# A four-attention transformer on one core: keys, heads and norms rearranged between its attentions

## The chip, the cores and the metric

The kernel runs on one core of a Trainium2 chip. Its engines are TensorE (PE in the profile), VectorE (DVE), ScalarE (ACT), GpSimd (POOL) and SyncE (SP, which here only issues DMAs); each runs its own instruction stream, and streams meet by semaphores only. The metric is the device time of one execution in microseconds, lower is better. Time before: 2822.0 us, the median of 3 runs (2814.44 to 2823.01).

## What is computed

Two blocks of a transformer on x of shape (1024 tokens, 128), all in float32, 16 heads of 8 columns each, and a context of 6404 rows of 128. Cut to what matters:

```
x = x + cross(norm(x), ctx, mask)            # cross0: 6404 keys, masked, Wproj, bproj
z = norm(x);  a = norm(z)*g1+b1
z = z + self(a) @ Wo                         # self0: 1024 keys
t = norm(z)*g2+b2
x = x + z + top2_experts(t)                  # 8 experts, 64 hidden columns each
z = norm(x)
z = norm(self(z, causal) + z)*g1+be1         # self1
z = norm(cross(z, ctx) + z)*g2+be2           # cross1: 6404 keys, unmasked
z = norm(relu(z@Wf1+bf1)@Wf2+bf2 + z)*g3+be3
x = x + z
x = x + top2_experts(norm(x)) + shared_expert(norm(x))
```

Every attention is softmax(q kT / sqrt(8)) v by heads; every norm is over the 128 columns.

## The kernel before

Everything is written out by hand for each engine, in one block; the order of the work is the order of the code. Tokens lie on partitions in 8 tiles of 128 (x, z, xn); "turned" they lie in xT, 128 columns by 1024 tokens, in two halves of 512.

**Projections.** projection_plan lists an attention's jobs: key jobs of up to 512 columns (13 for a cross attention, 2 for a self attention), then two query jobs. Each job is one TensorE product into PSUM (project), and is then split into three bfloat16 parts that add up to the float32 value: the parts by ScalarE (L829 to 836), the rests by VectorE, the third part by GpSimd (L657, L661). SyncE stores the parts to DRAM (store_parts, L448 for keys and L452 for queries, six stores per query job) and waits for all of them (all_stored, L457). cross1's key jobs go the way called "aside", in which ScalarE copies the product and GpSimd takes the first rest too; TensorE issues them right behind self1, ScalarE runs them (split of n_k_jobs) ahead of the norm that follows self1.

**Staging.** stage loads a head's parts from DRAM into one of 4 slots of k_stages and q_stages: two sides of 64 partitions, per side three loads of keys (L469 for a cross attention, L521 for a self attention) and one or two of queries (L472, L475, L523). SyncE stages four times ahead of an attention's first pass, and then once per pass. GpSimd copies the head's values into v_stage (stage_values, L667).

**A cross attention** has 32 passes, 16 heads by 2 halves of the queries. In a pass TensorE computes the scores twice: by queries (pass_a, 28 units), from which VectorE takes maxima (take_max, L1122) out of PSUM banks 0 to 3 in turn, and by keys (pass_b), from which ScalarE takes exponentials (L925) out of banks 4 to 6; products with the values (values_step) go to bank 7. Units of pass_a run some 40 ahead of the step that needs them. A pass's negated maxima (L1132) are split by GpSimd (split_maxima, L719 to L722), turned by TensorE (turn_maxima), copied by ScalarE to max_rows and put into the query stage by SyncE (put_maxima, L483). The end of a pass: ScalarE copies bank 7 to acc_out (evacuate, L914) once the copy before has been moved, and SyncE moves it to scratch in 8 DMAs (store_out, L496). GpSimd sums the four parts of all heads (sum_first after pass 16, sum_second at the end), VectorE takes reciprocals and products into attT and marks each half as attended. The self attentions (short_attention) do two heads per pass, 16 passes; their copies (L871) go through DRAM (store_out, L545) and come back by two loads, the last one after the last pass (load_out, L552).

**Between attentions.** TensorE multiplies attT by the output weights (out_tiles) or turns it back (turn_back, for self1 and cross1, which have no output weights); VectorE adds the result; layer_norm takes statistics of all 8 tiles (L1006), var_eps (L1011), waits for ScalarE's square root (L793), and applies them (L1016), with gain and bias where there are any (L1001); turn transposes 8 tiles (L1316), and turned copies half 0 by ScalarE (L799) and half 1 by VectorE (L1028). The expert layers compute the gate (L1234 copies its logits), choose two experts, turn the coefficients and run units of 128 hidden columns by half: products for coefficients (spread) and hidden columns into PSUM, an activation, products on VectorE, and at the end the down products of all tiles (out_tiles) behind the last unit. All TensorE products stand at L1308, the helper mm. At the start GpSimd writes constants, then clears q_stages (L639) and v_stage (L643) in long memsets; after cross0 it clears the query stages again (clear_queries, L767).

## Time and profile before

| | |
|---|---|
| Runs, median of 3 | 2822.0 us (2814.44 to 2823.01) |
| The profiled execution, own time | 2820.49 us |
| its span in the profile | 2818.9 us |
| TensorE (PE), busy | 2377.8 us, 84% |
| VectorE (DVE), busy | 2337.7 us, 83% |
| ScalarE (ACT), busy | 2154.4 us, 76% |
| GpSimd (POOL), busy | 250.3 us, 9% |
| Granted TensorE clock, mean | 0.928 |

The stages, in us from the start of the span: projection of cross0 to about 95, cross0 to 1106, self0 1167 to 1346, its experts, self1 1454 to 1618, cross1 1696 to 2705, then the feed-forward layer, the last experts and the store. The busy shares are means over all of these. A row of the timeline tells when an operation began, how long it took, its engine and line, what it writes and reads, how often in a row it ran, and in brackets how long the engine had stood idle and what ended that; "SPq" is SyncE's issuing of DMAs, "PEld" the loading of weights.

### The profile page before, as it was taken

The page shows a single profiled execution, that of the slowest core. Times are in us where ns is not written, and L with a number is a line of the kernel's source. Part 1 is how long each engine was busy: PE and PEld are TensorE (multiplying, and loading weights), DVE is VectorE, ACT ScalarE, POOL GpSimd, SP SyncE. Part 2 cuts the span into 40 slices and gives each one's busy share as a digit, 9 for nine tenths or more (in the row PEclk, how much of TensorE's full clock was granted, in tenths as well). Part 3 has the DMA queues.
Part 4 walks back from the last instruction along what each step waited for, and adds up shares of the span by engine and source line. Part 5 has one row for each costly group of instructions (what it writes and reads, how often), then busy time and mean ns, then how long its engine had stood idle before and what let it go on. Part 6 is the DMA issues. An engine that isn't in the chain of part 4 may idle for free.

```text
span 2818.9 us, 58993 instructions
## 1 busy us (share of the span) xinstructions
PE 2377.8 (84%) x23115; PEld 748.0 (27%) x23115; DVE 2337.7 (83%) x2590; ACT 2154.4 (76%) x4095; POOL 250.3 (9%) x684
## 2 busy tenths in 40 slices
PE   3499999999999996498458827999999999999955
PEld 2222222222222221122222213222222222222223
DVE  7599999999999993597446438999999999999825
ACT  3189999999999996299116733999999999999941
POOL 4001101001000001000010040000000100000000
PEclk8699999999999998599669957999999999999987
DMA  4211111111111100210121131111111111111000
GB/s 140 72 31 42 35 50 44 31 40 31 28 41 30 29 19 5 68 40 23 34 68 40 51 107 38 29 41 29 29 41 29 30 41 29 31 40 28 6 5 8
DMA packets 75974, 109.23 MB, mean 39 GB/s; under 512 B 16964, under 2 KB 55672, under 8 KB 75704
## 3 DMA queue, kind: packets, MB, share of 16 engines
q1 hardware_dynamic: 73912, 101.10, 12.4%
q0 software_dynamic: 1792, 4.37, 0.9%
q8 instruction: 189, 3.10, 0.5%
q14 instruction: 81, 0.66, 0.1%
HBM read 73.93 MB, written 22.42 MB: 34 GB/s over the span
## 4 chain that ended last, share of the span: by engine, by line
PE 66%; DVE 18%; ACT 6%; SPq 4%; issue 3%; DMA 3%; POOL 1%; ACTq 0%; POOLq 0%; DVEq 0%
PE ps L1308 65%; DVE maxima L1122 12%; ACT probs L925 4%; ACT probs L881 1%; DVE maxima L1077 1%; SPq L452 1%; DVE scratch L1001 1%; POOL probs L661 1%; SPq L521 1%; DMA o_self<-acc_out 1%; DMA q_stages<-q_cross 1%; PE ps L1316 0%; DVE stats L1006 0%; DVE z L1016 0%; POOL probs L657 0%
## 5 line engine op out<-in xcount | busy, mean ns | idle before, releaser
L1122 DVE TENSOR_REDUCE maxima<-ps 128x1 f32<-128x920 f32 x1792 | 1888.8, 1113 | 102.5 <-PE ps L1308 102.5
L925 ACT ACTIVATE probs<-ps 128x512 f32<-128x512 f32 (+1 forms) x3264 | 1761.2, 594 | 146.6 <-PE ps L1308 146.2
L1308 PE MATMUL ps<-probs,v_stage 128*16 128x256 f32 x14208 | 1158.9, 393 | 0.6 <-ACT acc_out L914 0.4
L1308 PE MATMUL ps<-k_stages,q_stages 64*128 64x460 bf16 (+2 forms) x4032 | 756.3, 373 | 192.2 <-DMA q_stages<-q_cross 68.0
L1308 PE MATMUL ps<-q_stages,k_stages 64*128 64x512 bf16 (+1 forms) x3712 | 725.3, 381 | 46.0 <-ACT probs L881 18.6
L1308 PEld LDWEIGHTS ps<-k_stages,q_stages 64*128 64x128 bf16 x4032 | 193.4, 93 | 1050.0 <-issue 510.2
L1308 PEld LDWEIGHTS ps<-probs,v_stage 128*16 128x16 f32 x14208 | 236.8, 94 | 410.8 <-issue 361.4
L1077 DVE TENSOR_REDUCE maxima<-ps 128x2 f32<-128x1024 f32 (+1 forms) x224 | 240.1, 1108 | 96.1 <-PE ps L1308 92.1
L881 ACT ACTIVATE probs<-ps 128x512 f32<-128x512 f32 x448 | 224.1, 554 | 67.3 <-PE ps L1308 66.2
L1308 PEld LDWEIGHTS ps<-q_stages,k_stages 64*128 64x128 bf16 x3712 | 187.3, 93 | 279.1 <-ACT probs L925 69.8
L1001 DVE TENSOR_TENSOR scratch<-scratch 128x512 f32<-128x512 f32 x14 | 15.2, 1134 | 155.4 <-DMA scratch<-acc_out 91.1
L846 ACT ACTIVATE by_key<-ps 128x512 f32<-128x512 f32 (+1 forms) x30 | 17.5, 583 | 150.1 <-PE ps L1308 150.1
L667 POOL COPY v_stage<-by_key 128x400 f32<-128x400 f32 x64 | 33.1, 516 | 991.4 <-PE ps L1308 873.4
L793 ACT ACTIVATE std<-var_eps 128x8 f32<-128x8 f32 x9 | 1.9, 208 | 117.7 <-DVE var_eps L1011 117.7
L719 POOL CAST half_parts<-neg_max 128x4 bf16<-128x4 f32 x64 | 11.9, 186 | 852.3 <-DVE neg_max L1132 794.5
L1001 DVE TENSOR_TENSOR probs<-ps,probs 128x512 f32<-128x512 f32 x36 | 24.9, 692 | 38.3 <-ACT probs L966 12.7
L1316 PE MATMUL ps<-ident,z 128*128 128x128 f32 x32 | 7.9, 426 | 49.4 <-DVE z L1001 25.9
L1316 PE MATMUL ps<-ident,xn 128*128 128x128 f32 x24 | 5.9, 426 | 43.9 <-DVE xn L1001 23.5
L914 ACT ACTIVATE acc_out<-ps 128x512 f32<-128x512 f32 x64 | 38.2, 597 | 2.4 <-PE ps L1308 2.4
L661 POOL TENSOR_TENSOR probs<-probs 128x512 bf16<-128x512 f32 (+1 forms) x23 | 26.0, 1141 | 153.5 <-ACT probs L836 153.5
L799 ACT ACTIVATE xT<-ps 128x512 f32<-128x512 f32 x7 | 4.2, 597 | 35.5 <-PE ps L1316 35.5
L1001 DVE TENSOR_TENSOR z<-ps,z 128x512 f32<-128x512 f32 x10 | 6.9, 690 | 28.7 <-PE ps L1308 24.8
(211 smaller groups left out, 916.2 us busy)
## 6 DMA issues: line engine op xcount, KB each, us to landing
q_stages<-q_cross SPq DMA_DIRECT2D x256, 48.0 KB, 4.6
k_stages<-k_cross SPq DMA_DIRECT2D x64, 150.2 KB
k_stages<-k_cross SPq DMA_DIRECT2D x64, 150.0 KB
k_cross<-probs SPq DMA_DIRECT2D x24, 384.0 KB, 2.7
scratch<-acc_out SPq DMA_DIRECT2D x512, 16.0 KB
k_stages<-k_cross SPq DMA_DIRECT2D x64, 100.1 KB
k_stages<-k_cross SPq DMA_DIRECT2D x64, 100.0 KB
q_stages<-q_self SPq DMA_DIRECT2D x32, 192.0 KB
```

The costliest lines, as they stand in the source:

```text
L452: sp.dma_start(a.q_dram[:, term * E:(term + 1) * E, c0:c0 + n], src[:, part, 0:n]).then_inc(done, DMA)
L521: sp.dma_start(k_stage(a, slot)[base + row:base + row + parts_ * E, :], a.k_dram[0:parts_, h * E:(h + 1) * E, :]).then_inc(done, DMA)
L661: nc.gpsimd.tensor_tensor(a.parts[:, b, 2, 0:n], a.rest[:, b, 0:n], a.parts[:, b, 1, 0:n], ALU.subtract).then_inc(sem("split_part3"), 1)
L667: nc.gpsimd.tensor_copy(v_stage[:, par, 0:full, 0:E], src[:, 0:full, :]).then_inc(sem(a.name + "_v_staged"), 1)
L846: last = nc.scalar.activation(by_key[:, t:t + full, :], src[:, 0:full, :], ACT.Copy)
L881: return nc.scalar.activation(probs[:, i % a.p_slots, low:BANK], ps[:, b_bank(a, use), low:BANK], ACT.Exp, scale=float(E) ** -0.5)
L914: nc.scalar.activation(acc_out[:], ps[:, ACC_BANK, :], ACT.Copy).then_inc(sem(a.name + "_acc_copied"), 1)
L925: return nc.scalar.activation(probs[0:m, probs_slot(a, j, i), :], ps[0:m, b_bank(a, use), :], ACT.Exp, scale=float(E) ** -0.5)
L1001: return nc.vector.tensor_tensor(out_, a, b, op)
L1077: nc.vector.tensor_reduce(pair_maxima[:, j % 2, :, qt % QT, c // BANK], ps[:, A_BANK + 2 * (g % 2):A_BANK + 2 * (g % 2) + 2, 0:n], AX_X, A ...
L1122: nc.vector.tensor_reduce(maxima[:, at, seg:seg + 1], ps[:, A_BANK + 2 * (g % 2):A_BANK + 2 * (g % 2) + 2, 0:a.segment], AX_XY, ALU.max).t ...
L1308: return nc.tensor.matmul(out_, lhsT, rhs, start=start, stop=stop)
```

## The change

It does the following; arithmetic stays the same but for the order of some sums.

1. cross1's 13 key jobs leave the place behind self1. Each becomes an item of cross0's list of maxima: passes 16 to 28 have one each (project into the next bank pair of pass_a, a VectorE copy to early_whole, four GpSimd operations into three parts, one SyncE store). The "aside" way goes away. SyncE issues the key loads of cross1's first four stagings once self1's scores are done, ahead of cross1's query stores.
2. The last head of each cross attention and the last two of each self attention don't go through scratch. At a fixed step of the last pass and behind it (take_late), TensorE multiplies acc_out by a small matrix late_out, that holds the output weights (or an identity) and a column of ones; VectorE takes a reciprocal and adds the result to x or z (add_late, add_late_values). The sums over the heads before are made during the last pass. Half 0 of a cross attention is finished at step 10 of its last pass (at_end).
3. Norms, turns, query projections, expert units and the output products go by halves of the tokens, with a semaphore for each half; ScalarE takes the square root of half 0 ahead of a cross attention's last copy.
4. The first two units of the expert layers are issued before the coefficients, and a down product starts once its own half of the units is done.
5. The first staging of each attention is shared: side 0 is issued by SyncE, side 1 by ScalarE, which waits for the stores by itself.
6. At the start GpSimd runs 4 memsets and 16 selects for late_out ahead of its long memsets; the loads of late_out join the weight loads.
7. Self attentions' jobs come in the order key, query, key, query.

Cut to its core:

```diff
-    k_mode = "masked" if a.masked else "aside" if a.keys > 2 * BANK else "plain"
-    k_jobs = [("k", k_mode, c, min(BANK, a.keys - c)) for c in range(0, a.keys, BANK)]
+    k_jobs = [("k", "masked" if a.masked else "plain", c, min(BANK, a.keys - c)) for c in range(0, a.keys, BANK)]
     q_jobs = [("q", "plain", c * BANK, BANK) for c in range(HALVES)]
-    a.jobs = k_jobs + q_jobs
+    if a.masked:
+        a.jobs = k_jobs + q_jobs
+    elif a.cross:
+        a.jobs, a.early_jobs = q_jobs, k_jobs
+    else:
+        a.jobs = [job for pair in zip(k_jobs, q_jobs) for job in pair]
...
+    a.half_step = 10
+    a.early_from, n = 16, len(a.max_units)
+    early = {(a.early_from + 2 + i) * n + 4: i for i in range(early_jobs)}
+    a.items, a.items_with = [], [0]
+    for v in range(a.n * n):
+        if v in early:
+            a.items.append(("key", early[v]))
+        a.items.append(("max", v))
+        a.items_with.append(len(a.items))
+    a.key_item = {i: k for k, (kind, i) in enumerate(a.items) if kind == "key"}
+    a.job_banks = [i % 3 for i in range(ceil_div(keys, BANK) + HALVES)] if masked else [6, 0]
...
+        def wait_stored(queue, a):
+            for i in range(max(0, len(a.jobs) - SPLITS), len(a.jobs)):
+                queue.wait_ge(stored(a, i), stored_count(a, i))
+        def stage_side_keys(queue, a, j, side):
+            h, _ = a.passes[j]
+            base, (first, count) = side * SIDE, a.side_keys[side]
+            for row, parts_ in ((0, 3), (3 * E, 2), (5 * E, 1)):
+                queue.dma_start(k_stage(a, j % a.ring)[base + row:base + row + parts_ * E, 0:count],
+                                a.k_dram[0:parts_, h * E:(h + 1) * E, first:first + count]).then_inc(staged(a, j), DMA)
...
+                def store_early(i):
+                    _, _, c0, n = cross1.early_jobs[i]
+                    sp.wait_ge(sem("early_split"), i + 1)
+                    sp.dma_start(cross1.k_dram[:, :, c0:c0 + n].rearrange("a p c -> p a c"),
+                                 early_parts[:, :, 0:n]).then_inc(sem("early_stored"), DMA)
...
-                store_out(a.n - 1)
+                    if j - a.early_from in a.key_item:
+                        store_early(j - a.early_from)
...
+                def load_out(half):
+                    rows = slice(0, (H - 2) * E)
                     for kind, dst in enumerate((o_parts, den_parts)):
-                        sp.dma_start(dst[rows], a.o_dram[:, kind, rows].rearrange("g p q -> p g q")
-                                     ).then_inc(sem(a.name + "_out_in"), DMA)
...
+                    if 1 <= j < a.n - 1:
                         store_out(j - 1)
-                sp.wait_ge(sem(a.name + "_acc_free"), (a.n - 2) * 4 * DMA)
-                load_out(0, H - 2)
-                store_out(a.n - 1)
-                sp.wait_ge(sem(a.name + "_acc_free"), a.n * 4 * DMA)
-                load_out(H - 2, H)
+                    if a.n - 3 <= j < a.n - 1:
+                        sp.wait_ge(sem(a.name + "_acc_free"), j * 4 * DMA)
...
+                if a is self1:
+                    sp.wait_ge(sem("self1_scores"), 2 * len(self1.all_steps) + self1.n)
+                    sp.wait_ge(sem("early_stored"), cross1.n_k_jobs * DMA)
+                    for j in range(cross1.ring):
+                        stage_keys(cross1, j)
...
+            for late in late_out.values():
+                link(nc.gpsimd.memset(late[:], 0.0))
+            for late in (late_out["cross0"], late_out["cross1"]):
+                for g in range(4):
+                    col = late[:, 0, :] if late.shape[2] == VCOLS else late[:, 0, D:D + 1]
+                    first = 32 * g + (0 if late.shape[2] == VCOLS else E)
+                    link(nc.gpsimd.affine_select(out=col, in_=col, compare_op=ALU.not_equal, fill=1.0, base=-first,
+                                                 pattern=[[-1, col.shape[1]]], channel_multiplier=1))
...
+                def split_early(i):
+                    n = cross1.early_jobs[i][3]
+                    whole, rest, parts = early_whole[:, 0:n], early_rest[:, 0:n], early_parts[:, :, 0:n]
+                    pool.wait_ge(sem(a.name + "_max_read"), a.key_item[i] + 1)
+                    if i >= 1:
+                        pool.wait_ge(sem("early_stored"), i * DMA)
+                    link(nc.gpsimd.tensor_copy(parts[:, 0, :], whole))
+                    link(nc.gpsimd.tensor_tensor(rest, whole, parts[:, 0, :], ALU.subtract))
+                    link(nc.gpsimd.tensor_copy(parts[:, 1, :], rest))
+                    nc.gpsimd.tensor_tensor(parts[:, 2, :], rest, parts[:, 1, :],
+                                            ALU.subtract).then_inc(sem("early_split"), 1)
...
+            def layer_norm(*halves):
+                for b in halves:
+                    count[b] += 1
+                    tiles = slice(b * QT, (b + 1) * QT)
+                    act.wait_ge(sem(f"ln_variance{b}"), count[b])
+                    nc.scalar.activation(std[:, tiles], var_eps[:, tiles], ACT.Sqrt).then_inc(sem(f"ln_std{b}"), 1)
...
+                layer_norm(0)
                 evacuate(a.n - 1)
...
+                split(a, 0, len(a.jobs))
+                wait_stored(act, a)
+                if a is cross0:
+                    act.wait_ge(sem("rows_in"), ROWS_IN * DMA)
+                    stage_side_keys(act, a, 0, 1)
+                if a is self0:
+                    act.wait_ge(sem("q_cleared"), 2)
+                if a.cross:
+                    stage_side_queries(act, a, 0, 1)
+                else:
+                    stage_pair_side(act, a, 0, 1)
                 if a.cross:
                     cross_attention(a)
...
+            def add_late(a, nth, b, bank, dst, done):
+                heads = late_out[a.name].shape[1]
+                per_bank = 2 // heads
+                dve.wait_ge(sem(a.name + "_late"), nth + 1)
+                banks = ps[:, bank:bank + QT // per_bank, 0:2 * (D + 1)]
+                tiles = banks.rearrange("p b (k c) -> p b k c", k=2)
+                rec = late_rec[:].rearrange("p t s e -> p (t s e)")[:, 0:QT * heads].rearrange(
+                    "p (b k o) -> p b k o", k=2, o=1)
+                link(nc.vector.reciprocal(rec, tiles[:, :, :, D:D + 1]))
+                for s_ in range(heads):
+                    for t in range(QT):
+                        at = t * heads + s_
+                        to = dst[:, b * QT + t, :]
+                        last = nc.vector.scalar_tensor_tensor(to, tiles[:, at // 2, at % 2, 0:D], rec[:, at // 2, at % 2, :],
+                                                              to, ALU.mult, ALU.add)
+                    if s_ + 1 < heads:
+                        link(last)
+                last.then_inc(sem(done), 1)
+                dve.wait_ge(sem(done), nth + 1)
...
+            def take_late(a, copies, bank):
+                pe.wait_ge(sem(a.name + "_acc_copied"), copies)
+                rhs = late_out[a.name][:].rearrange("p s c -> p (s c)")
+                cols = rhs.shape[1]
+                per_bank = QT if QT * cols <= BANK else 2 // late_out[a.name].shape[1]
+                for t in range(QT):
+                    at = t % per_bank * cols
+                    last = mm(ps[:, bank + t // per_bank, at:at + cols], acc_out[:, t * P:(t + 1) * P], rhs)
+                last.then_inc(sem(a.name + "_late"), 1)
...
+                    if kind == "key":
+                        if i == 0:
+                            pe.wait_ge(sem("weights_in"), DMA * (len(loads) - n_first))
+                        _, _, c0, keys = cross1.early_jobs[i]
+                        mm(ps[:, A_BANK + 2 * (g % 2), 0:keys], flat(W["k_cross1"]),
+                           ctxT[:, c0:c0 + keys]).then_inc(sem(a.name + "_max_scores"), 1)
...
+                        if j == a.n - 1 and t == a.half_step:
+                            at_end(0)
+                at_end(1)
...
+            def cross0_end(b):
+                is_attended(cross0, b)
+                rows = P if b == 0 else P - E
+                out_tiles(b, b, [(attT, W["o_cross0"][:])], rows)
+            cross_attention(cross0, ctxT, kv[:, D:2 * D], cross0_end)
+            take_late(cross0, cross0.n, 2)
+            for b in range(HALVES):
+                turn(b, xn, 3, b)
+                half_turned(b, 2)
+                project(self0, W["q_self0"][:], W["k_self0"][:], xT, 2 * b, 2 * b + 2)
             short_attention(self0, xT, W["v_self0"][:])
...
+            for u in range(2):
+                moe0_up(u)
+            turn_coef(0, 6)
             for u in range(CX * HALVES):
-                c, half = u // HALVES, u % HALVES
                 if u >= 2:
                     pe.wait_ge(sem("moe0_hidden"), u - 1)
+                    moe0_up(u)
+                moe0_coef(u)
+            for b in range(HALVES):
+                pe.wait_ge(sem("moe0_hidden"), (b + 1) * CX)
+                out_tiles(b, b, [(hidden[:, c, :], W["down0"][:, c, :]) for c in range(CX)])
```

## Rows read from the trace of the kernel before

**Rows 1.** busy time by stages: PE, PEld, DVE, ACT, POOL; then clock, DMA share
```profile
131.00:1062.00 931.00, 893.45 (x9328) 256.29 (x9328) 911.72 (x895) 856.73 (x1617) 75.26 (x225) 0.99 0.13 34
...
1672.00:1697.00 25.00, 0.53 (x4) 0.13 (x4) 0.69 (x1) 1.20 (x3) 2.27 (x2) 0.55 0.40 113
```

**Rows 2.** timeline of the start: begin, length, engine, line, operation
```profile
10.65 6.91 DVE L1011 TENSOR_SCALAR var_eps<-mean_var 128x8 f32<-128x8 f32 x1
...
12.59 3.54 POOL L639 MEMSET q_stages<- 128x2048 f32 x2
```

**Rows 3.** costliest groups by form, VectorE and GpSimd, whole span
```profile
L1122 DVE TENSOR_REDUCE maxima<-ps 128x1 f32<-128x920 f32 x1792 | 1888.8, 1113 | 102.5 <-PE ps L1308 102.5
...
L1028 DVE COPY xT<-ps 128x512 f32<-128x512 f32 x7 | 4.8, 692 | 15.0 <-PE ps L1316 15.0
...
L661 POOL TENSOR_TENSOR probs<-probs 128x512 bf16<-128x512 f32 x22 | 25.3, 1163 | 152.9 <-ACT probs L836 152.9
```

**Rows 4.** timeline of TensorE, two stretches that price its products
```profile
1410.78 7.41 PE L1308 MATMUL ps<-w_down,probs 128*128 128x128 f32 x64 [1.41 <-DVE probs L1001]
...
2732.52 8.88 PE L1308 MATMUL ps<-xT,w_f 128*128 128x512 f32 x16 [0.85 <-DVE xT L1028]
```

**Rows 5.** timeline, first cross attention's end to the second norm's turn
```profile
1105.93 0.60 ACT L914 ACTIVATE acc_out<-ps 128x512 f32<-128x512 f32 x1 [1.21 <-PE ps L1308]
...
1106.55 5.29 SPq L496 DMA_DIRECT2D scratch<-acc_out  x8
...
1125.50 1.64 DVE L1006 BATCH_NORM_STATS2 stats<-x 128x6 f32<-128x128 f32 x8
...
1140.54 0.69 DVE L1028 COPY xT<-ps 128x512 f32<-128x512 f32 x1 [2.13 <-PE ps L1316]
```

**Rows 6.** timeline, query stores and staging ahead of self0
```profile
1149.71 7.93 SPq L452 DMA_DIRECT2D q_self<-probs  x12
...
1159.58 1.94 SPq L521 DMA_DIRECT2D k_stages<-k_self  x3
...
1167.24 0.61 PE L1308 MATMUL ps<-k_stages,q_stages 64*128 64x512 bf16 x2 [20.19 <-DMA q_stages<-q_self]
```

**Rows 7.** timeline, self0's end, its gate, and self1's first score
```profile
1345.74 0.60 ACT L871 ACTIVATE acc_out<-ps 128x512 f32<-128x512 f32 x1 [1.17 <-PE ps L1308]
...
1353.68 0.78 SPq L552 DMA_DIRECT2D scratch<-o_self  x2
...
1385.39 0.23 DVE L1234 COPY logits<-ps 128x64 f32<-128x64 f32 x1 [3.67 <-PE ps L1308]
...
1453.84 0.29 PE L1308 MATMUL ps<-k_stages,q_stages 64*128 64x128 bf16 x2 [19.94 <-DMA q_stages<-q_self]
```

**Rows 8.** timeline, self1's end to the last attention's fourth staging
```profile
1617.16 0.60 ACT L871 ACTIVATE acc_out<-ps 128x512 f32<-128x512 f32 x1 [1.06 <-PE ps L1308]
...
1659.80 0.21 ACT L793 ACTIVATE std<-var_eps 128x8 f32<-128x8 f32 x1
...
1673.83 7.68 SPq L452 DMA_DIRECT2D q_cross<-probs  x12
...
1683.37 1.94 SPq L469 DMA_DIRECT2D k_stages<-k_cross  x3
...
1696.47 0.95 PE L1308 MATMUL ps<-k_stages,q_stages 64*128 64x460 bf16 x4 [25.04 <-DMA q_stages<-q_cross]
...
1710.64 1.66 SPq L475 DMA_DIRECT2D q_stages<-q_cross  x2
```

**Rows 9.** DMA issues from 1712 to 1724 us: KB each, us to landing
```profile
q_stages<-q_cross SPq DMA_DIRECT2D x1, 48.0 KB, 14.6
```

**Rows 10.** timeline, the last attention's end and the last layer
```profile
2704.05 0.60 ACT L914 ACTIVATE acc_out<-ps 128x512 f32<-128x512 f32 x1 [1.21 <-PE ps L1308]
...
2779.79 0.60 PE L1308 MATMUL ps<-scratch,spread 24*128 24x512 bf16 x1 [0.51 <-DVE scratch L1207]
...
2805.20 1.16 PE L1308 MATMUL ps<-w_xdown,probs 128*128 128x128 f32 x8 [1.41 <-DVE probs L1001]
```

670 lines of the change are left out of this document (386 added, 284 removed).

## The prediction

> **What bounds the kernel now.** I read the busy time by stages first. In the body of the first cross attention (131 to 1062 us) VectorE is busy 911.7 of 931 us and TensorE 893.5 [rows 1]: both are full, ScalarE nearly so, and the second cross attention looks the same. Between the attentions nothing is full: from 1672 to 1697 TensorE works 0.5 us of 25 and even the DMA engines only 0.40 [rows 1]. There one chain of dependent steps sets the time, handed from engine to engine. So an edit inside a cross attention costs what it adds to the two full engines, and an edit between them is worth what it takes off the chain. I went through the timeline of each gap and asked what each step waited for.
>
> The profiled execution took 2820.5 us around a span of 2818.9; the median of the three is 2822.0, 0.05% above. The sum is made against 2820.5.
>
> **The start (0 to 97 us).** The layer norm goes by halves, and GpSimd gets 4 memsets and 16 selects, each waited for, ahead of its long memsets. VectorE's small var_eps operation took 6.91 us, from 10.65 to 17.56, while GpSimd ran memsets back to back (one pair is 12.59 to 16.13) [rows 2]; it came through in the first gap. The new short instructions leave such gaps early, but they push the long memsets about 5 us later, where they stand against the norm's end or the mask operations. I take a gain of 2 us, with 5 either way. The Trainium skill (SBUF — State Buffer, Who interferes with whom) says that a VectorE operation in a two-port mode and a GpSimd one lock each other out for a whole instruction, whichever starts first; row and rule agree on the 6.91 us, and by the rule each long memset could cost its full length again, the third rival below.
>
> **Thirteen key jobs of the last attention, moved into the first.** Each is one product of 512 columns (two instructions) and one copy of 128x512 from PSUM put between the maxima, one per pass in passes 16 to 28. VectorE has 28 maxima of 1113 ns a pass, so it pays the copy in full, 0.69 us [rows 3]; TensorE pays about 1.1 us (sixteen such instructions took 8.88 [rows 4]) against some 0.6 us of slack per pass. I take 1.0 us each, 13 us in all; the ends are 0.69 (9 us) and 2.0 (26 us), if the double step also starves ScalarE. GpSimd's four operations of about 1.16 us [rows 3] and SP's one store per pass come after the pass's turn of the maxima, in time that both spend waiting; if that cover were gone, see the fourth rival.
>
> **Cross attention to self attention.** From the end of the last accumulator copy (1106.5) to the transposed input (1141.2) 34.7 us pass [rows 5]. The first 19.0, up to the statistics at 1125.50, are eight outgoing DMAs (5.29 us of issue), their landing, the partial sums, a reciprocal and the projection. The change sums 15 of 16 heads before the last pass has ended and multiplies the last head straight out of acc_out. In their place stand: 1.0 us for eight products put ahead of the last values (64 such take 7.41 [rows 4], 0.12 each), 0.7 because ScalarE now takes the first half's square root ahead of the copy, 1.0 because GpSimd's clearing of the query stages now falls on that norm, 1.3 for the late product and 1.4 for adding it. That leaves 13.6. Halving takes the first half's statistics and its turn out of the remaining 15.7: 1.9. Then 26.0 us to the first score at 1167.24 [rows 6]: twelve stores of queries take 7.93, and with the first half projected first the last six end 3.0 us earlier. Side 1 of the first staging goes to ScalarE: the staging takes 7.7 us from 1159.58 to the score, of which some 4.6 are issue (three loads take 1.94) [rows 6]; halving that could bring 0 to 2.3 us, and I take 1.0, since the transfers follow the issue closely. Sum 19.5, less 0.6 for four products in the last pass: **19 us**.
>
> **Self attention to the experts.** 1346.3 to the router's logits at 1385.4, 39 us [rows 7]. The last pass went through DRAM (second load issued at 1353.68) and then through sums and two reciprocals. Now 14 heads are summed while the last pass runs; the second half is ready about 1347.6, the products, the late heads (258 columns) and eight combining operations end near 1353, then half a statistics, two half norms with gain (5.2), a half turn and half the gate: logits near 1364. Gain 21 less 1 for the first late product inside the last pass: **20 us**. From there to the first score of the next attention, 1453.84 [rows 7], 68.4 us pass: two of the eight up-products run before the coefficients are there (2.4 net of a longer copy), the down-products of the first half don't wait for the last unit (1.41 us stood there [rows 4]), additions and statistics by halves 1.7, stores 2.2, staging 1.0: **9 us**.
>
> **Into the last attention.** The copy ends at 1617.8, the first score comes at 1696.5: 78.7 us. ScalarE, full of key jobs, reached the norm's square root only at 1659.80; then came the query stores at 1673.83 and the staging from 1683.37 [rows 8]. The key jobs are gone from here, so the norm's chain alone would have the query stores issued by about 1645.7 (load of the heads' sums landed 1616, sums 6.2, turn and late part 4.3, statistics and norm 4.2 for the half, turn 1.8, product 2.1, split 3.3, stores 7.7) and the first score at 1650.5. But SP first issues 24 loads of staged keys, from about 1617. Four whole stagings took from 1683.37 to about 1726: the last issue is at 1710.64, for 1.66 us, and lands 14.6 us on [rows 8, 9]. That is 42 us for 3.2 MB at a share of 0.3 to 0.4 of the engines, so bytes don't spread well. Keys are three quarters of the bytes: 32 us, and up to 42 if they set it all. I take 38, nearer the upper end since the first staging alone took 13.1 us, to the score at 1696.47, against under 5 of issue [rows 8]. For the same reason I take 0 for splitting the first staging of the first attention between two queues. The query stores queue behind it: landed about 1660, first score 1661.5: **35 us** gained, between 29 and 46. The Trainium skill (DMA: Bandwidth & Descriptors, Why a DMA increments its semaphore by 16 and not by 1) says that such a load uses the largest number of engines up to 16 that divides both slowest dimensions. That would be 3, 2 or 8 for these key loads, the lowest-numbered each time, and the rows' low share agrees. By it the keys of both queues meet on the same engines.
>
> **The end.** 2704.7 to 2732.5 [rows 4, 10] loses the last DMA trip: the new chain is late product 2.2, adding 1.1, statistics 1.35, first half norm 2.7, half turn 1.8, so the first layer begins near 2714, 18.6 us earlier. The feed-forward and expert layers by halves: its two halves with a turn between cost 1.5 back, the gate 1.0, additions and norms beside products 5 gained; two shared-expert units run before the coefficients that came at 2779.79, so eight instead of ten units stand before the last products at 2805.20 [rows 10], 5 gained with the overlap of the last halves. Less 0.6 in the last pass: **26 us**.
>
> **Sum.** 2 - 13 + 19 + 20 + 9 + 35 + 26 = 98 us; 2820.5 - 98 = 2722.5, and 0.05% more for the median: 2723 to 2724. I forecast **2723 us** (2700 to 2742 by this case's own bounds), chance 0.57.
>
> **The rivals.**
> First, the preloaded keys don't hold the queries up: the stores overtake them or the keys are fast alone. For it: between attentions the engines are busy a third of their time. Against: landings of 14.6 us behind other loads [rows 9]. The full 46 us come: 2712. Chance 0.15.
> Second, a key job breaks the step in which TensorE, VectorE and ScalarE lock together and costs two maxima, 2.2 us. For it: three nearly full engines, three PSUM banks between two of them. Against: two double steps per pass are there already. 2739. Chance 0.14.
> Third, the long memsets fall on the norm or the mask work at the start: 5 us lost in place of 2 gained: 2730. Chance 0.07.
> Fourth, and on the other side: SP waits for each split key job before it stages on. By my reckoning the copy is done 21 us into a 30 us pass, the split by 26, and SP needs 41 at the latest for the next maxima (some 10.8 us ahead of them: eight stores, 5.29 [rows 5], and a staging like it). If GpSimd came so late that SP got free beyond 41, every further us would cost 13; from 48.5 it eats up the whole 98, and at 51 the time is 2853. Against it stand 15 us of margin. Chance 0.02.
> Fifth, the change doesn't do what it says: doing halves turns one hand-over into two, TensorE falls to its lower clock in the shorter stretches, and each of four gaps gives 4 us less: 2739. Chance 0.05.
>
> **How the numbers follow.** The low end, 2700, takes cheap key jobs (4), the fast keys (11) and a good start and split staging (8). The high end, 2752, takes the second rival (13 to 16), slow keys (6) and a poor start (7). Outside lie the slower rival and unforeseen cases, and combinations of the fast bounds. A measurement can tell about 0.3%, 8.5 us. All cases but the fourth are faster by more: faster 0.97, same 0.01, slower 0.02.
>
> **What the profile would show.** Passes 16 to 28 of the first cross attention about 1 us longer than 30.1, the others unchanged. One accumulator copy at the end of each attention followed by four product pairs and no outgoing DMA. About 42 us from the first copy to the next score, 19 to the first logits. In the last gap SP issues 24 key loads from 1617 minus what was gained before, and the query stores land late; if first scores come within 3 us of the stores' issue, the first rival is right. The first staging of cross0 no shorter than 12 us. What makes the forecast wrong: a pass stretched by more than 2 us, or a wait of VectorE on GpSimd after the norms.

## The result, and the profile after

The changed kernel takes 2730.5 us (median of 4 runs, 2729.7 to 2734.6) against 2821.3 for the kernel before (median of 4): a ratio of 0.9686, interval 0.9667 to 0.9704. The forecast was 2723, range 2700 to 2752 (the prediction also names 2742 as an upper bound; its own sum of the high end gives 2752, and the result lies within both). The span of its profiled execution is 2728.0 us against 2818.9, 90.9 us less; 98 were forecast.

I cut both spans at the same events: the first score of each attention (rows "MATMUL ps<-k_stages,q_stages") and the end of its last copy to acc_out. Positive is a gain.

| stretch | before | after | gain | forecast |
|---|---|---|---|---|
| start to cross0's first score | 96.96 | 95.37 | 1.6 | 2 |
| cross0, first score to last copy | 1009.57 | 1025.11 | -15.5 | -15.3 (the jobs -13, its last pass -2.3) |
| last copy to self0's first score | 60.71 | 41.23 | 19.5 | 21.3 (19 with the last pass's -2.3) |
| self0 | 179.10 | 180.32 | -1.2 | -1 |
| last copy to the router's logits | 39.05 | 21.47 | 17.6 | 21 (20 with self0's -1) |
| logits to self1's first score | 68.45 | 60.91 | 7.5 | 9 |
| self1 | 163.92 | 164.75 | -0.8 | 0 |
| last copy to cross1's first score | 78.71 | 41.31 | 37.4 | 35 |
| cross1 | 1008.18 | 1010.59 | -2.4 | -0.6 |
| last copy to the end | 114.25 | 86.94 | 27.3 | 26.6 (26 with cross1's -0.6) |

Here are the rows of the changed kernel's timeline (start, length, engine, line, operation, and in brackets the idle time before it and what ended it). First the start, which answers [rows 2]:

```profile
9.62 0.85 DVE L1143 TENSOR_SCALAR var_eps<-mean_var 128x4 f32<-128x4 f32 x1
...
19.53 3.54 POOL L757 MEMSET q_stages<- 128x2048 f32 x2
...
21.35 3.41 DVE L1203 TENSOR_SCALAR probs<-probs 128x512 bf16<-128x512 uint8 x1
```

VectorE's var_eps took 0.85 us instead of 6.91; the long memsets, which stood beside it before, now begin at 19.53. There they meet another VectorE operation, the third of the mask: it took 3.41 us, to 24.76, about where the memsets end (in the kernel before it took 0.42). Second, one of the 13 passes with a key job, in cross0:

```profile
674.44 1.12 PE L1525 MATMUL ps<-ctxT,w_k_cross 128*128 128x512 f32 x2
675.60 0.69 DVE L1271 COPY z<-ps 128x512 f32<-128x512 f32 x1 [0.71 <-PE ps L1525]
676.12 3.23 ACT L1045 ACTIVATE probs<-ps 128x512 f32<-128x512 f32 x6 [1.04 <-PE ps L1525]
```

TensorE's product takes 1.12 us, VectorE stood idle for 0.71 before its copy of 0.69, ScalarE for 1.04 before its next exponential. Third, cross0's end and the way to self0, which answer [rows 5, 6]:

```profile
1119.79 0.20 ACT L921 ACTIVATE std<-var_eps 128x4 f32<-128x4 f32 x1 [1.75 <-DVE var_eps L1143]
1119.90 0.58 ACT L1034 ACTIVATE acc_out<-ps 128x512 f32<-128x512 f32 x1
1120.53 1.16 PE L1525 MATMUL ps<-late_cross,acc_out 128*128 128x129 f32 x8 [1.55 <-ACT acc_out L1034]
1123.11 0.87 DVE L1137 BATCH_NORM_STATS2 stats<-x 128x6 f32<-128x128 f32 x4
...
1138.22 1.06 PE L1531 MATMUL ps<-ident,xn 128*128 128x128 f32 x4
1139.38 0.69 DVE L1166 COPY xT<-ps 128x512 f32<-128x512 f32 x1 [3.78 <-PE ps L1531]
...
1154.28 2.27 SPq L501 DMA_DIRECT2D k_stages<-k_self  x3
1154.31 1.89 ACTq L501 DMA_DIRECT2D k_stages<-k_self  x3
1161.71 0.61 PE L1525 MATMUL ps<-k_stages,q_stages 64*128 64x512 bf16 x2 [19.60 <-DMA q_stages<-q_self]
```

No DMA stands between the copy and the late product any more (SPq is SyncE's issuing, ACTq ScalarE's). The next rows are self0's end and the logits, against [rows 7]:

```profile
1341.43 0.60 ACT L993 ACTIVATE acc_out<-ps 128x512 f32<-128x512 f32 x1 [1.17 <-PE ps L1525]
...
1341.51 2.29 DVE L1342 SCALAR_TENSOR_TENSOR z<-ps,late_rec,z 128x128 f32<-128x128 f32 x8
1343.85 3.15 PE L1525 MATMUL ps<-w_o_self,attT 112*128 112x128 f32 x16 [2.48 <-DVE z L1342]
...
1363.50 0.22 DVE L1433 COPY logits<-ps 128x64 f32<-128x64 f32 x1 [1.96 <-PE ps L1525]
```

And the way into the last attention, against [rows 8]:

```profile
1587.11 19.67 SPq L487 DMA_DIRECT2D k_stages<-k_cross  x24
1588.56 0.60 ACT L993 ACTIVATE acc_out<-ps 128x512 f32<-128x512 f32 x1 [1.06 <-PE ps L1525]
...
1611.02 12.36 SPq L544 DMA_DIRECT2D q_cross<-probs  x12
1628.61 0.32 SPq L494 DMA_DIRECT2D q_stages<-q_cross  x1
...
1630.47 0.95 PE L1525 MATMUL ps<-k_stages,q_stages 64*128 64x460 bf16 x4 [21.86 <-DMA q_stages<-q_cross]
```

SyncE issues 24 loads of staged keys, then the twelve stores of queries: these take 12.36 us instead of 7.68, and land 5.2 us after their last issue (at 1628.61, when the staging starts) instead of 1.9.

### The profile page after: what moved, and what is told of

Its sections match the earlier page's. It is cut to its first block, busy times and chain, and to the rows that moved or that the text cites. A ratio compares the mean times of both kernels' runs of the same rounds, so it can differ in the third digit from the quotient of the medians.

```text
span 2728.0 us, 59209 instructions
## 1 busy us (share of the span) xinstructions
PE 2385.4 (87%) x23163; PEld 751.5 (28%) x23163; DVE 2352.7 (86%) x2668; ACT 2134.1 (78%) x4065; POOL 275.0 (10%) x740
## 4 chain that ended last, share of the span: by engine, by line
PE 68%; DVE 18%; ACT 5%; issue 3%; SPq 3%; DMA 3%; POOL 0%; ACTq 0%; DVEq 0%
PE ps L1525 67%; DVE maxima L1261 12%; ACT probs L1045 4%; SPq L544 1%; DVE maxima L1220 1%; ACT probs L1003 1%; DVE scratch L1131 1%; SPq L501 1%; DVE stats L1137 0%; DMA q_stages<-q_cross 0%; PE ps L1531 0%; DVE z L1131 0%; DMA q_stages<-q_self 0%; DMA scratch<-o_self 0%; DMA o_self<-acc_out 0%
## 5 line engine op out<-in xcount | busy, mean ns | idle before, releaser
L1131 DVE TENSOR_TENSOR scratch<-scratch 112x512 f32<-112x512 f32 (+1 forms) x14 | 13.6, 982 | 64.4 <-DMA scratch<-acc_out 39.7
L800 POOL CAST max_parts<-neg_max 128x8 bf16<-128x8 f32 x32 | 6.1, 190 | 209.2 <-DVE neg_max L1231 154.9
L770 POOL TENSOR_TENSOR probs<-probs 128x512 bf16<-128x512 f32 x10 | 11.3, 1152 | 149.1 <-ACT probs L959 149.1
L1166 DVE COPY xT<-ps 128x512 f32<-128x512 f32 x7 | 4.8, 692 | 23.6 <-PE ps L1531 23.6
```

Source lines behind the costliest of these rows:

```text
L1131: return nc.vector.tensor_tensor(out_, a, b, op)
```

## The experiments

All kernels below are the changed kernel with the edit shown ("..." marks what is left out). Most were executed once, which the text says by "one execution"; their stretches are read from their traces, cut as in the table above. How much a stretch moves by itself is told by the kernels whose code is the same there: the start takes 95.2 to 95.8 us, cross0 1024.8 to 1026.1, the way to self0 40.4 to 41.5, self0 179.2 to 180.4, self0 to the logits 21.5 to 23.9, the logits to self1 58.9 to 63.9, self1 163.3 to 172.1 (see the clock, at the end), the end 85.9 to 86.9. So stretches say more than totals, and only differences outside these bounds say something.

**How many stagings of keys may run ahead of the queries?** Three kernels, none, one and two ahead instead of four; the rest of the keys follow with the queries of their own staging:

```diff
-                    for j in range(cross1.ring):
+                    for j in range(1):            # 0, 1 or 2
                         stage_keys(cross1, j)
...
                     if a is cross0:
                         stage_keys(a, j, (0, 1) if j else (0,))
+                    elif j >= 1:                  # 0, 1 or 2
+                        stage_keys(a, j)
                     stage_queries(j)
```

> The changed kernel, but the key loads of the last attention's first four stagings are issued behind the query stores, each with the queries of its own staging, none ahead. Theory A (key loads in the queue hold the query stores up; in the changed kernel the twelve stores take 12.36 us to issue and land 5.2 us later, against 7.68 and 1.9 before): the stores are back at 7.7 and 1.9 us, and the first staging, with its keys, takes 13.1 us as before the change, so the first score comes 44.5 us after the last copy of self1 instead of 41.3. Theory B (the stores are slow by themselves): they take 12.4 us again and the score comes at about 54 us. Theory C (staging keys ahead costs nothing and gains all it can): the score at 52 us or more.

> Keys of one staging ahead of the query stores, those of the other three behind, each with its queries. Theory A: the 6 loads have drained before the stores begin at about 1611 us; stores 7.7 us, landed 1.9 us later, first score 1.9 us behind, 33 us after the last copy of self1 instead of 41.3, so 8 us gained, unless the later keys come late for their passes. Theory B: 41 us again.

> Keys of two stagings ahead of the query stores. Four stagings took 42 us before, so 12 key loads take some 16 us from 1587 us and have drained by 1604 to 1608. Theory A: first score 33 to 35 us after the last copy of self1, ratio to the kernel before 0.9655 to 0.966 instead of 0.9686. Theory B: 41 us and 0.9686.

| ahead | query stores, issue | last issue to staging | last copy to first score | time |
|---|---|---|---|---|
| 0 | 7.67 | 1.9 | 41.5 | 2729.9 (one execution) |
| 1 | 7.68 | 1.8 | 32.3 | 2720.7 (one execution) |
| 2 | 7.66 | 1.8 | 29.0 | 2723.0, ratio 0.9645 (0.9626 to 0.9664) |
| 4 (the change) | 12.36 | 5.2 | 41.3 | 2730.5, ratio 0.9686 (0.9667 to 0.9704) |

The query stores' rows with two ahead:

```profile
1594.81 7.51 SPq L487 DMA_DIRECT2D k_stages<-k_cross  x12
1615.73 7.66 SPq L544 DMA_DIRECT2D q_cross<-probs  x12
```

Theory A holds: with up to 12 key loads ahead the stores take their old time, with 24 they are held up, by 4.7 us in their issue and 3.4 in their landing, and the first score comes some 9 us later. Four stagings ahead gained no more in this stretch than none (41.3 and 41.5 us): the 9 us that the first staging saves, the other three cost. So the 37 us that the change gained here don't come from loading keys early. With none ahead I had expected 44.5 and got 3 us less; that wasn't followed. (The 29.0 with two ahead flatters it: there self1's last two passes were 6.5 us longer, so that its sums were further on when the copy came.)

**Is the first staging faster from two queues?** ScalarE's part is taken out, SyncE issues both sides:

```diff
-                wait_stored(act, a)
-                if a is cross0:
-                    act.wait_ge(sem("rows_in"), ROWS_IN * DMA)
-                    stage_side_keys(act, a, 0, 1)
...
-                    for side in range(a.sides if pair else 1):
+                    for side in range(a.sides):
                         stage_pair_side(sp, a, pair, side)
```

> SyncE issues both sides of every first staging, as before the change; the rest is the changed kernel. My theory: each of the two self attentions' first scores comes 1.0 us later, cross0's and cross1's 0 to 0.5 us: 2 to 3 us in all. Rival (issue sets the staging's time, as each side is 2.3 us of issue): 2.3 us later in each self attention, as much or more in cross0: 5 to 7 us in all. Second rival (the transfers set it): no difference.

2725.9 us in one execution, less than the change. The first scores come after 93.64 us (95.37 with two queues) at the start, 41.20 (41.23) ahead of self0, 41.66 (41.31) ahead of cross1. The second rival holds in the gaps: the issue doesn't set the time there, which leaves the transfers. At the start sharing even cost 1.7 us (the first version below, again with one queue, has 93.75). The side's three key loads take ScalarE 3.22 us, SyncE's three beside it 1.96, and SyncE goes straight on to the second staging:

```profile
81.33 1.96 SPq L487 DMA_DIRECT2D k_stages<-k_cross  x3
81.35 3.22 ACTq L487 DMA_DIRECT2D k_stages<-k_cross  x3
84.84 4.02 SPq L487 DMA_DIRECT2D k_stages<-k_cross  x6
...
95.37 0.95 PE L1525 MATMUL ps<-k_stages,q_stages 64*128 64x460 bf16 x4 [43.79 <-DMA q_stages<-q_cross]
```

```profile
81.32 3.86 SPq L487 DMA_DIRECT2D k_stages<-k_cross  x6
87.26 3.74 SPq L487 DMA_DIRECT2D k_stages<-k_cross  x6
```

The first rows are the change, the second the one-queue kernel, whose second staging begins at 87.26 instead of 84.84. That the second staging's early loads take the place of the first one's last ones is a reading of these rows; it was not tried by itself.

**What is the halving worth?** Half 0's turn also waits for half 1's norm:

```diff
                 pe.wait_ge(sem(f"ln_out{b}"), ln)
+                if b == 0:
+                    pe.wait_ge(sem("ln_out1"), ln)
```

> The changed kernel, in which the turn of half 0 also waits for the norm of half 1, at all seven norms: what is left of the halving is the order of the work. My theory (the halves are worth what half 0's turn starts earlier): 2.8 us at each of the norms with gain and bias (ahead of self0, of the first gate, of the last attention and of the feed-forward layer) and 1.2 us at those without (ahead of self1 and of the last gate), so some 13 us in all, 2.8 of it between cross0 and self0 and 2.8 ahead of the last attention. Rival (the second half sets the time anyway, so the first one's lead is lost behind it): under 4 us in all.

Span 2739.1, 11.1 us longer (one execution). By stretches: ahead of self0 +2.9, ahead of the logits +3.8, from there to self1 +3.5, the end +3.4, ahead of cross1 -0.2. So the rival (under 4 us in all) falls. The two in the middle move by up to 5 us by themselves, but together they take 89.7 us here and 82.4 to 85.7 in the kernels with the same code, so that about 4 us of their 7.3 at least are the halves'. One place differs, and tells most: ahead of cross1 the query stores could begin only at 1622.64, 7.8 us after the last key load instead of 4.2, took 8.83 us instead of 12.36, and the first score came no later. So what stands last there is the keys' transfer, not the norm: stores that began 2.9 us later behind the copy landed no later.

```profile
1595.56 19.30 SPq L487 DMA_DIRECT2D k_stages<-k_cross  x24
1622.64 8.83 SPq L544 DMA_DIRECT2D q_cross<-probs  x12
1636.69 0.32 SPq L494 DMA_DIRECT2D q_stages<-q_cross  x1
```

**What is the removed trip through DMA worth?** Each attention's last copy is moved out once more, and its late product waits for the landing:

```diff
+                store_out(a.n - 1)
...
                 pe.wait_ge(sem(a.name + "_acc_copied"), copies)
+                if copies == a.n:
+                    pe.wait_ge(sem(a.name + ("_out_in" if a.cross else "_acc_free")),
+                               (a.n * 8 if a.cross else (a.n - 1) * 4) * DMA)
```

> The changed kernel, but the last copy of each attention is also moved out by its DMAs (eight for a cross attention, four for a self attention), and the late product of that copy waits until they have landed: the outgoing trip is back, the sums are not. My theory: each cross attention's end gets 5.3 us of issue and about 2 of landing longer, each self attention's 2.5 and about 2, in all 7.3 + 7.3 + 4.5 + 4.5 = 23.6 us. Rival (the late product isn't what the norm waits for, the sums of the other heads are): under 5 us in all.

Span 2752.9, 24.9 us longer (one execution) against 23.6 expected: behind cross0 8.8, behind cross1 7.9, behind self1 5.6, and behind self0 0.8, which is no more than that stretch moves by itself. Of the 8.8 behind cross0, 7.1 lie between the copy's end and the late product, and the product itself took 2.06 us instead of 1.16 after TensorE had stood idle for 8.65. Only self0's late product doesn't wait for the trip: the output products of the other heads keep TensorE busy until 1347.0, 5 us behind the copy, in the change's row above. The remaining 2 us lie in self1's body, which varies by itself.

**What is the price of a key job?** First with a product of 128 columns, then with a copy of 128:

```diff
-                        mm(ps[:, A_BANK + 2 * (g % 2), 0:keys], flat(W["k_cross1"]),
-                           ctxT[:, c0:c0 + keys])...
+                        mm(ps[:, A_BANK + 2 * (g % 2), 0:128], flat(W["k_cross1"]),
+                           ctxT[:, c0:c0 + 128])...
```

```diff
-                    n = cross1.early_jobs[i][3]
+                    n = cross1.early_jobs[i][3] if i == 0 else 128
```

> The key jobs inside cross0 with a product of 128 columns instead of 512; the copy, the split and the store keep their size. Left out: three quarters of the last attention's key projection, so that its keys are wrong. The passes with a key job are 31.16 us long, those without 30.11. Theory A (VectorE pays its copy of 0.69 us, and 0.36 us is its wait for a product that is longer than a score's): the pass is 30.8 us, 4 to 4.5 us less in all. Theory B (the double step costs as such, whatever its size): 31.1 us again.

> The key jobs inside cross0 with VectorE's copy cut to 128 columns after the first job; product, split and store keep their size. Left out: three quarters of each copy but the first, so that the keys are wrong. Theory A: the copy falls from 0.69 to some 0.2 us and the passes to 30.6 to 30.7 us. Theory C (TensorE's product of 1.02 us is the price, and the copy lies beside it): 31.1 us again. Theory B: 31.1 us.

```profile
670.95 0.17 DVE L1280 TENSOR_REDUCE neg_max<-maxima 128x4 f32<-128x28 f32 x1
674.34 0.69 DVE L1271 COPY z<-ps 128x512 f32<-128x512 f32 x1
...
701.58 0.17 DVE L1280 TENSOR_REDUCE neg_max<-maxima 128x4 f32<-128x28 f32 x1
```

```profile
671.74 0.17 DVE L1280 TENSOR_REDUCE neg_max<-maxima 128x4 f32<-128x28 f32 x1
675.76 0.29 DVE L1271 COPY z<-ps 128x128 f32<-128x128 f32 x1 [0.71 <-PE ps L1525]
...
702.94 0.17 DVE L1280 TENSOR_REDUCE neg_max<-maxima 128x4 f32<-128x28 f32 x1
```

A pass lasts from one neg_max row to the next: 30.63 us with the narrow product (0.49 us of TensorE), 31.20 with the narrow copy (0.29 us of VectorE), 31.16 in the change, 30.11 without a job. Theory C holds. The job costs what TensorE's product lasts, 0.5 us for 0.49 and 1.05 for 1.12, and cutting VectorE's copy from 0.69 to 0.29 us gained nothing: the row of the change shows VectorE waiting 0.71 us for that product, and a shorter copy doesn't bring the product earlier. (Both kernels leave out three quarters of the work that they narrow, so their keys are wrong.)

**Why have the self attentions grown, and was it the load ahead of the maxima?** The first load of the heads is issued behind the last pass's maxima:

```diff
+                    if j == a.n - 2:
+                        sp.wait_ge(sem(a.name + "_acc_free"), (a.n - 3) * 4 * DMA)
+                        load_out(0)
                     if 1 <= j < a.n - 1:
                         store_out(j - 1)
-                    if a.n - 3 <= j < a.n - 1:
-                        sp.wait_ge(sem(a.name + "_acc_free"), j * 4 * DMA)
-                        load_out(j - (a.n - 3))
+                    if j == a.n - 2:
+                        sp.wait_ge(sem(a.name + "_acc_free"), (a.n - 2) * 4 * DMA)
+                        load_out(1)
```

> The changed kernel, but in the self attentions the first load of the summed heads is issued behind the maxima of the last pass instead of ahead of them. In the changed kernel TensorE waits 1.21 us for those maxima in self1 at 1577.80, in one profile of another version 2.40 us, and after that second one its granted clock is 0.51 to 0.54 for the rest of the pass. My theory (the load of 448 KB, queued first, holds the maxima up, and that costs what the bodies of the self attentions have grown by): self0's body from 180.3 to some 179.2 us, self1's from 164.8 to 172 down to some 163.7, the gate no later. Rival (the late product inside the last pass is what the bodies have grown by): no difference.

Wrong, and the other way: 2733.4 us in one execution, self0's body 184.4 instead of 180.3, self1's 169.8 instead of 164.8. The load now stands right ahead of the copy's way out:

```profile
1572.84 0.91 SPq L648 DMA_DIRECT2D scratch<-o_self  x2
1573.80 2.49 SPq L641 DMA_DIRECT2D o_self<-acc_out  x4
...
1581.26 0.60 ACT L996 ACTIVATE acc_out<-ps 128x512 f32<-128x512 f32 x1 [3.98 <-DMA o_self<-acc_out]
1582.40 0.61 PE L1528 MATMUL ps<-q_stages,k_stages 64*128 64x512 bf16 x2 [5.17 <-ACT probs L1006]
```

ScalarE waited 3.98 us for that store to land before it could copy the next pass, and TensorE, behind it, 5.17. In self0 the same waits are 2.73 and 3.69 us; the stretch behind it is 2.2 us shorter in turn (19.28), since its sums are further on. The load is two transfers of 448 KB, which land 5.1 us after their issue, and the four stores of 32 KB queued behind them came late. Ahead of the maxima the load goes with a wait of TensorE of 1.2 us (at 1577.80 in the change), and of 2.0 to 2.5 in eight of the nine other kernels with that code. Whether the self attentions have grown at all stays open: the kernel before has 179.1 and 163.9 us, the kernels with the change's code 179.2 to 180.4 and 163.3 to 172.1.

**Why did the stretch behind self0 miss?** Its output products go to banks 6 and 7, so that they need not wait for the first late addition:

```diff
-                add_result("self0", b, b, z, z)
+                add_result("self0", b, 6 + b, z, z)
...
-            pe.wait_ge(sem("self0_late_added"), 1)
             for b in range(HALVES):
                 is_attended(self0, b)
-                out_tiles(b, b, [(attT, W["o_self0"][:])], (H - 2) * E)
+                if b == 1:
+                    pe.wait_ge(sem("self0_acc_copied"), self0.n)
+                out_tiles(b, 6 + b, [(attT, W["o_self0"][:])], (H - 2) * E)
+            pe.wait_ge(sem("self0_late_added"), 1)
```

> The changed kernel, but self0's output products go to banks 6 and 7 instead of 0 and 1, so that TensorE needn't wait until VectorE has added the first late heads (2.29 us of additions, 2.48 us of TensorE's waiting at 1343.85). My theory of the missing 3.6 us behind self0: from the last copy to the logits some 1.5 to 2.4 us less than the 21.5 of the changed kernel. Rival (the norm waits for the second late product, which waits for the last copy): under 0.5 us.

```profile
1341.91 2.05 PE L1525 MATMUL ps<-w_o_self,attT 112*128 112x128 f32 x16
1342.49 2.29 DVE L1342 SCALAR_TENSOR_TENSOR z<-ps,late_rec,z 128x128 f32<-128x128 f32 x8
1344.83 2.01 PE L1525 MATMUL ps<-late_self,acc_out 128*128 128x258 f32 x8 [0.88 <-DVE z L1342]
```

19.19 us from the last copy to the logits instead of 21.47 (2724.7 us in one execution): the 2.3 us of the upper end, and below all seven kernels with the old banks (21.5 to 23.9). TensorE's products now lie beside VectorE's additions. They are shorter too, 2.05 us for 3.15: in the change TensorE waits 2.48 us ahead of them and its granted clock is 0.64 from 1344 to 1346 and 0.50 from 1346 to 1348, here it doesn't wait and the clock stays at 1.00. How much of the 2.3 us is the overlap and how much the clock wasn't separated.

**Two versions made of these.** The first has one queue for staging, keys of one staging ahead, the later loads, banks 6 and 7, and in cross0's end the statistics of half 0 ahead of the second addition. The second adds ScalarE as the issuer of the last query job's six stores:

```diff
+                i = len(a.jobs) - 1
+                _, _, c0, n = a.jobs[i]
+                act.wait_ge(sem("split_part3"), a.jobs_before + i + 1)
+                for term, part in enumerate(Q_PARTS):
+                    act.dma_start(a.q_dram[:, term * E:(term + 1) * E, c0:c0 + n],
+                                  a.parts[:, i % SPLITS, part, 0:n]).then_inc(stored(a, i), DMA)
```

> A version made from what the runs showed: one queue for the first stagings, keys of one staging ahead, first load of the self attentions' heads later, self0's products in banks 6 and 7, and in cross0's end the first half's statistics ahead of the second half's addition (so that the square root isn't late for the last copy: 0.9 us). Expected gain over the changed kernel: 1.7 at the start, 0.9 ahead of self0, 1.2 and 1.2 in the self bodies, 1.5 to 2.4 ahead of the gate, 9 ahead of the last attention: 15 to 17 us, so 2713 to 2716 us, ratio to the kernel before 0.962 to 0.963. If the parts get in each other's way, 2720.

> The version before this one, in which ScalarE also issues the six stores of the last query job of every attention, beside SyncE's six of the first. Theory A (issue by one queue sets the time between the last split and the staging: twelve stores take 7.7 to 7.9 us): 2 to 4 us less in each of the three gaps between attentions and up to 2 at the start, 6 to 12 us in all: 2703 to 2709 us. Theory B (the DMA engines set it, as with the shared staging, which brought nothing in the gaps and cost 1.7 us at the start): no gain, 2713 to 2716 us.

The first takes 2725.4 us (ratio 0.9662, 0.9649 to 0.9675), 10 more than hoped. Its self bodies are 185.0 and 171.6 us, 4.7 and 6.9 more than in the change. At self0 that is what the later loads cost in their own run (4.1). At self1 it isn't only they: the second version, with the same code there, has 165.8. The other parts came as expected: 93.75 us at the start, cross0's last copy no longer waits for the square root (it does in neither version), 18.23 to the logits. The 30.48 ahead of cross1 are flattered by the long self1, as above.

The second takes 2715.8 (0.9624, 0.9611 to 0.9637), the fastest of all, and better than both kernels. That isn't the stores' gain alone: of the 8.9 us between the two profiled executions 5.9 are self1's body, in which the code is the same. Nor does the total tell the theories apart, as it is 9.6 us below the first version (theory A) but stands where theory B had put it; the stretches do. The first score at the start comes at 90.19 instead of 93.75, and ahead of cross1 it takes 28.04 instead of 30.48, but some of that is given back in the attentions behind: they take 1.4 and 1.5 us longer to their last copies. Ahead of self0 it takes 42.07 instead of 41.38, nothing gained:

```profile
1606.50 3.89 SPq L544 DMA_DIRECT2D q_cross<-probs  x6
1607.61 4.03 ACTq L1075 DMA_DIRECT2D q_cross<-probs  x6
1613.82 0.78 SPq L494 DMA_DIRECT2D q_stages<-q_cross  x2
```

```profile
1139.95 3.81 SPq L544 DMA_DIRECT2D q_self<-probs  x6
1142.65 4.71 ACTq L1075 DMA_DIRECT2D q_self<-probs  x6
1150.26 1.95 SPq L501 DMA_DIRECT2D k_stages<-k_self  x3
```

Ahead of cross1 both queues work at once and the staging begins at 1613.82, 7.3 us after the first store. Ahead of self0 ScalarE's stores begin only at 1142.65, and the staging starts 10.3 us after SyncE's first store, as with one queue. At the start ScalarE issues its six from 60.36 on, 12 us ahead of SyncE's first at 72.39, so that the gain there is also that of an earlier start. So theory A holds at two places of four (at self1 the stretch is 1.1 us shorter, well within what it moves by itself). The Trainium skill (DMA: Bandwidth & Descriptors, Issuing engines are not separate DMA queues) says that issuing from several engines at once saves only the sequencers' time, which is usually small against the transfer. The runs agree for staging, where nothing was gained; for the twelve stores of 128 KB it is 3.6 and 2.4 us up to the first score, at two places. The second version without the later loads wasn't tried.

## Why the prediction was right, point by point

**The start**: 1.6 for 2, and partly by luck. The 6.91 us of var_eps are 0.85, as [rows 2] let one expect, and the turned input came 6.7 to 7.1 us earlier. The third rival fell by its sum but not by its mechanism: a mask operation took 3.41 us beside the long memsets instead of 0.42, and by the end of the key projections 2.8 us of the gain were left. Of the 3.3 that one queue would have given (93.64), sharing the first staging cost 1.7.

**The key jobs**: 12.7 us for 13 (cross0 up to the last pass), the passes 1.05 us longer for 1.0. But the working was wrong: I had VectorE pay its copy in full, since it is the fullest engine by [rows 1, 3], and TensorE have 0.6 us of slack per pass. The narrow copy saves nothing and the narrow product half: what a job costs is TensorE's product, 1.11 us by [rows 4] and without the slack. Right size, wrong engine, so the agreement is luck. The second rival (2.2 us a job) fell, and so did the fourth: no pass with a key job grew by more than 1.1 us.

**Cross0 to self0**: 16.7 us for 19 (with the 2.8 that the last pass grew by). The trip was worth what its return costs, 8.8 us, and up to the statistics the sum was right (13.5 us for 13.6, the last pass taken off). The step that failed is the 1.9 us that halving was to take off up to the second half's turn. From the first statistics behind the copy to the end of xT it took 15.7 us before and 17.0 after. VectorE's part of it, to the last operation of the norm, is 12.5 us for 12.9, since VectorE still has both halves to do; then turn 1 waits from 1135.60 to 1138.22, behind the four products of half 0 on TensorE. And the square root ahead of the copy cost 0.9 us (copy at 1119.90, values done at 1118.98), for 0.7, since VectorE added both halves before it took the first one's statistics; the 1.0 us for GpSimd's clearing wasn't seen: it ended at 1119.32, ahead of var_eps. The queries' stores and staging gave 4.4 us for 4.0, but the 1.0 of it for the shared staging was nothing by the one-queue run, so that the stores' part was larger than the 3.0 I gave it.

**Self0 to the logits**: 16.4 us for 20 with self0's body. The mis-sized term is "ready at 1347.6, all combined near 1353": it took 9.8 us from the copy instead of 6.7. I had given the first late addition (2.29 us) as cover to the products, but they wait for it, as they take its banks. The kernel with other banks gave 2.3 us of it back. The change's own trace is the best of the seven with that code (21.5 to 23.9 us), so that on average the miss is larger.

**Logits to self1**: 7.5 us for 9, and self1's body is 0.8 longer. Kernels with the same code take 58.9 to 63.9 us here, a gain of 4.5 to 9.5, so that the terms of this sum (products, additions, stores, staging) are neither confirmed nor refuted.

**Into cross1**: 37.4 us for 35. The first rival (keys don't hold queries) fell: the runs with 0, 1, 2 and 4 stagings ahead show the hold-up directly. I had the stores landed 43 us after the first key load and the score 43.7 us after the copy; it was 41.5 and 41.3. So the size, 38 us for four stagings of keys, was right to some 3 us. What the prediction doesn't say is that the same 37 us come with no keys ahead at all. They come from what left this gap: the outgoing trip (5.6 us by its return) and, for the most part, the key jobs, whose share no run took by itself.

**The first staging on two queues**: nothing for the 1.0 us ahead of self0 (ahead of self1 none can be told from what that stretch moves by itself), and 1.7 lost at the start, where I had said 0.

**Cross1 and the end**: 24.9 us for 26. The late product and half 0's early end did what was said: the first layer begins 8.3 us behind the copy, for 9.3, and 27.9 before; cross1's body is 2.4 us longer, 0.9 of it in the last pass and 1.5 in the first two, and the latter stays open.

Sum: 1.6 - 12.7 + 16.7 + 16.4 + 7.5 - 0.8 + 37.4 + 24.9 = 91.0 us, for 98. No term is off by more than 3.6 us; at the start and in the key jobs two errors cancelled.

## What to carry to other kernels

Between two full stages the time is a chain of hand-overs: a DMA trip taken out of it is worth its issue and landing in full, if the chain's other arm isn't later (behind self0 it was, and the trip cost 0.8 us there, nothing that can be told from chance, instead of 5.6 to 8.8). A transfer moved ahead of the chain isn't free: it should be only as much as drains before the chain's own stores come, here one or two stagings of four. And a job put into a body whose engines run in lock-step cost its length on one of them, here not the one with the highest busy share. Which one it is was told by cutting the job in two ways.

## What the runs showed of the hardware

TensorE's granted clock falls from 1.00 (2.4 GHz) to its lower level of 1.2 GHz for a while near self1's end in every trace, but not at one place. In the change it is 0.66 from 1565 to 1570, ahead of which TensorE waited for nothing longer than 0.96 us, and 1.00 in the last two passes, where it waited 1.21 us for the last maxima. In the eight kernels in which that wait was 2.0 to 2.5 us the clock fell behind it, and from the last copy but two to the last it took 15.6 to 20.5 us, against 13.9 in the change (which lost 1.2 in the pass before these). The kernel with two stagings ahead is the worst: its wait at 1581.42 was 2.40 us, and the clock is 0.54 and 0.51 in the stretches that follow. Busy time by stretch (start:end, length, PE, PEld, DVE, ACT, POOL, granted clock, DMA share, GB/s), the change first:

```profile
1565.00:1570.00 5.00, 4.72 (x41) 1.24 (x44) 0.31 (x2) 3.12 (x8) 0.78 (x4) 0.66 0.05 15
...
1580.00:1590.00 10.00, 7.73 (x88) 3.59 (x88) 8.08 (x6) 7.41 (x16) 0.00 (x0) 1.00 0.39 101
```

```profile
1581.42 0.61 PE L1527 MATMUL ps<-q_stages,k_stages 64*128 64x512 bf16 x2 [2.40 <-DMA q_stages<-max_rows]
...
1580.00:1590.00 10.00, 7.90 (x50) 1.80 (x50) 6.86 (x7) 5.97 (x12) 0.00 (x0) 0.54 0.40 118
1590.00:1598.00 8.00, 8.00 (x60) 3.83 (x60) 5.93 (x8) 2.32 (x7) 0.00 (x0) 0.51 0.06 15
```

So a wait of some 2 us ahead of a body's last pass was followed by a loss of 1.7 to 6.6 us over the last two passes, the wait included; what sets its size wasn't tried.

The loads of staged keys leave the DMA engines idle for the most part: in the change, between 1587 and 1611, while 24 of them are issued and under way, the queue moves 1.80 MB at a share of 21% (75 GB/s). The query stores behind them run at a share of 0.48 from 1611 to 1624; with two stagings ahead, when the loads have drained, it is 0.64 from 1616 to 1625. The queue's row is packets, MB and share:

```profile
q1 hardware_dynamic: 365, 1.80, 21.0%
```
